# Sixteen prefilled row buffers, weight parts between the transposes, stored rows by the vector engine, and a dense product begun on three tiles

## What is computed

```python
def _gine_layer(x, src, dst, edge_attr, eps, We, be, W1, b1, gamma, beta, W2, b2):
    e = edge_attr @ We + be
    m = jax.nn.relu(x[src] + e)
    agg = jax.ops.segment_sum(m, dst, num_segments=x.shape[0])
    h = ((1.0 + eps) * x + agg) @ W1 + b1
    mu = jnp.mean(h, axis=0)
    var = jnp.mean(jnp.square(h - mu), axis=0)
    h = (h - mu) * jax.lax.rsqrt(var + BN_EPS) * gamma + beta
    h = jax.nn.relu(h)
    return jax.nn.relu(h @ W2 + b2)
...
for l in range(L):
    x = _gine_layer(x, src, dst, edge_attr, eps[l], We[l], be[l], W1[l], b1[l], gamma[l], beta[l], W2[l], b2[l])
```

## Time and profile before

| | |
|---|---|
| median of 3 runs | 971.86 us (967.61 to 972.33) |
| profiled execution | 970.5 us |
| its span on the core | 968.6 us |
| mean granted clock of PE | 0.921 |
| PE busy | 841.4 us, 87% |
| DVE busy | 712.1 us, 74% |
| ACT busy | 516.6 us, 53% |
| POOL busy | 281.5 us, 29% |

### The profile page before, as it was taken

The page is one execution under the profiler, slowest core; times in us unless marked ns, Lnnn a source line. Parts: engine busy times, 40 slices in busy tenths (PEclk is TensorE's granted clock), DMA queues, the critical chain, the costliest instruction groups (busy, mean ns, idle before and its releaser), DMA issues.

```text
span 968.6 us, 13328 instructions
## 1 busy us (share of the span) xinstructions
PE 841.4 (87%) x3561; PEld 603.7 (62%) x3561; DVE 712.1 (74%) x1275; ACT 516.6 (53%) x986; POOL 281.5 (29%) x245
## 2 busy tenths in 40 slices
PE   2989779887869789995999989999999999999796
PEld 2667345655647567773665865667656766658664
DVE  8997825765876677786888668976799758986535
ACT  2376103544646241514786567755677557764445
POOL 3000653865200000015352075502654045520000
PEclk9989657989969799997999999999999999999898
DMA  5412454676433312208676077841978138860101
GB/s 113 142 38 87 115 161 154 178 225 193 151 99 157 129 45 64 84 26 217 148 187 180 3 202 179 200 119 33 240 177 217 37 108 197 178 165 1 43 1 53
DMA packets 59286, 122.20 MB, mean 126 GB/s; under 512 B 9096, under 2 KB 22698, under 8 KB 59221
## 3 DMA queue, kind: packets, MB, share of 16 engines
q0 software_dynamic: 20048, 52.18, 22.6%
q1 hardware_dynamic: 36581, 64.56, 22.6%
q10 hardware_dynamic: 2592, 4.61, 1.3%
HBM read 105.60 MB, written 15.73 MB: 125 GB/s over the span
## 4 chain that ended last, share of the span: by engine, by line
PE 67%; DVE 17%; ACT 8%; issue 5%; another core or an unknown queue 2%; DMA 1%; SPq 0%; ACTq 0%; DVEq 0%
PE ps L996 15%; PE ps L973 10%; PE ps L671 9%; PE ps L1012 6%; PE ps L1028 6%; PE ps L797 4%; PE ps L862 3%; PE ps L919 3%; PE ps L776 2%; PE ps L663 2%; ACT slot_recs L1090 2%; PE ps L765 2%; DVE z_parts L1864 1%; DVE w L1391 1%
## 5 line engine op out<-in xcount | busy, mean ns | idle before, releaser
L996 PE MATMUL ps<-z_parts,onehot_dst 128*125 128x512 f32 x664 | 205.2, 414 | 5.6 <-DVE z_parts L1864 2.9
L1864 DVE SCALAR_TENSOR_TENSOR z_parts<-ps,z_parts 128x512 fp32r<-128x512 f32 x216 | 147.9, 688 | 43.4 <-ACT z_parts L1296 31.0
L671 PE MATMUL ps<-w,xT 128*125 128x512 f32 x660 | 174.7, 419 | 5.1 <-DVE w L1391 5.1
L1296 ACT ACTIVATE z_parts<-ps 128x512 fp32r<-128x512 f32 x216 | 128.7, 597 | 80.9 <-PE ps L973 66.9
L973 PE MATMUL ps<-x_parts,gather_lhs 128*128 x432 | 142.4, 415 | 22.5 <-DVE x_parts L1831 12.1
L996 PEld LDWEIGHTS ps<-z_parts,onehot_dst 128*125 128x125 f32 x664 | 110.0, 186 | 72.8 <-issue 55.0
L671 PEld LDWEIGHTS ps<-w,xT 128*125 128x125 f32 x660 | 129.8, 200 | 37.7 <-issue 6.8
L639 POOL DMA_INDIRECT queued<-node_rows,srci x60 | 96.0, 1600 | 93.7 <-ACT queued L1245 76.8
L653 POOL TENSOR_TENSOR work<-x_cur,be_rows 125x512 f32<-125x512 f32 x20 | 25.5, 1282 | 317.7 <-ACT x_cur L1059 188.9
L973 PEld LDWEIGHTS ps<-x_parts,gather_lhs 128*128 128x128 f32 x432 | 80.3, 193 | 56.5 <-issue 40.2
L633 POOL DMA_INDIRECT gathered<-rel_rows,rowi x79 | 85.7, 1084 | 51.4 <-DVE gathered_parts L1623 22.0
(11 more groups left out here) (275 smaller groups left out, 1154.7 us busy)
## 6 DMA issues: line engine op xcount, KB each, us to landing
w_stage<-in_weights SPq DMA_DIRECT2D x88, 256.0 KB
onehot_dst<-onehot_rows SPq DMA_DIRECT2D x80, 250.0 KB
onehot_rows<-onehot_dst ACTq DMA_DIRECT2D x18, 250.0 KB
gather_lhs<-edge_src_rows SPq DMA_DIRECT2D x8, 432.0 KB, 7.4
node_rows<-work SPq DMA_DIRECT2D x20, 160.0 KB, 2.0
queued<-node_rows,srci POOLq DMA_INDIRECT x116
node_rows<-work SPq DMA_DIRECT2D x20, 90.0 KB, 2.0
rel_rows<-rel_rows_out SPq DMA_DIRECT2D x10, 160.0 KB, 1.9
```

Of the source, the lines that this page charges most:

```text
L671: mm = pe.matmul(ps[0:R, bank, :], lt[:, a, k, n * R:(n + 1) * R], w[:, b, k, :], start=first and k == 0 and (a, b) == THREE[0], stop=last ...
L996: mm = pe.matmul(ps[0:R, d, :], S[:, j // SK % SR, j % SK, :], Z[:, g % ZR, a, :], start=False, stop=False, skip_group_check=True)
L1296: nc.scalar.activation(Z[:, g % ZR, HI, :], of, ACT.Relu).then_inc(z_hi, 1)
L1864: v.scalar_tensor_tensor(out=Z[:, g % ZR, LO, :], in0=of, scalar=0.0, in1=Z[:, g % ZR, HI, :].bitcast(F32), op0=ALU.max, op1=ALU.subtract) ...
```

## The change

It has four parts.

- **Sixteen prefilled buffers.** QR goes from 10 to 16; six more buffers lie in the second half of the adjacency's region, which the third network doesn't use. The first 16 fetched tiles of a layer are all prefilled by ACT and filled by adding DMAs; of the 13 after them every second one. `queue_set` runs 23 times a layer instead of 15, `queue_add` 6 times instead of 14. The sets of buffers 0 and 1 stand in the first dense product (SET_W1), those of 2 to 10 after the cast of the next layer's first weights (SET_W2), those of 11 to 15 at steps 2, 4, 6, 8, 10 of the pass (SET_AT).
- **Second weights among the transposes.** ACT's and DVE's parts of W 13 + 2l leave the pass and are made around the transposes of the last two row tiles. SP's load of W 14 + 2l, which needs their staging buffers, follows; the load of We's next row stands ahead of it.
- **Stored rows by DVE.** From the second layer on DVE writes relu(result) + be into H straight from PSUM, behind each low part; POOL does it only ahead of the first layer. ACT's X copy waits for that instead of for the low part.
- **First dense product begun on three row tiles.** PE transposes three tiles, does the first job, transposes the last two, and goes on.

```diff
-QR = 10
+QR = 16
+QL = 10
...
-EARLY = 10
+SET_W1, SET_W2 = 2, 11
+SET_AT = (2, 4, 6, 8, 10)
...
-W2_HIGH, W2_LOW = (24, 26, 28, 30), (28, 31, 34, 37)
...
-SETS = (TL + 1) // 2
-ADDS = TL // 2
+MIXED = TL // 2
+SETS = QR + (TL - QR + 1) // 2
+ADDS = TL - SETS
...
-        Q = [at(l_at, TF * P * 4 + 2048 * i, f"queued{i}", [P, D]) for i in range(QR)]
-        BEB = at(l_at, TF * P * 4 + 2048 * QR, "be_rows", [P, D])
-        WEB = at(l_at, TF * P * 4 + 2048 * (QR + 1), "we_rows", [P, D])
+        Q = [at(l_at, TF * P * 4 + 2048 * i, f"queued{i}", [P, D]) for i in range(QL)]
+        Q += [at(a_at, APAD * 4 + 2048 * i, f"queued{QL + i}", [P, D]) for i in range(QR - QL)]
...
+        def prefilled(k):
+            return k < QR or (k - QR) % 2 == 0
+
+        def sets(k):
+            return sum(prefilled(j) for j in range(k + 1))
+
+        def adds(k):
+            return k + 1 - sets(k)
...
+                if l < NL2 - 1:
+                    sp.wait_ge(q_set, SETS * (l + 1))
+                    sp.wait_ge(q_add, ADDS * (l + 1))
+                    web_load(l + 1)
                 w_load(14 + 2 * l)
                 if l < NL2 - 1:
                     for g in range(SR):
                         s_load(l + 1, g)
-                    sp.wait_ge(q_set, SETS * (l + 1))
-                    sp.wait_ge(q_add, ADDS * (l + 1))
-                    web_load(l + 1)
...
-                if k % 2 == 0:
-                    gp.wait_ge(q_set, SETS * l + k // 2 + 1)
+                if prefilled(k):
+                    gp.wait_ge(q_set, SETS * l + sets(k))
                     gp.indirect_dma_start(Q[k % QR][:, :], None, xb_d, row, compute_op=ALU.add)\
                         .then_inc(q_in[k % QR], 16)
                 else:
-                    if k >= QR:
-                        gp.wait_ge(z_made, l * TE + STEP[TF + k - QR] + 1)
+                    gp.wait_ge(z_made, l * TE + STEP[TF + k - QR] + 1)
...
+            gp.wait_ge(beb_in, 16)
+            for n in range(NT):
+                gp.wait_ge(x_made, XM_L3 - NT + n + 1)
+                gp.tensor_tensor(H[0:R, n, :], X[0:R, n, :], BEB[0:R, :], ALU.add).then_inc(xb_made, 1)
...
-                for n in range(NT):
+
+                def g_transposes(n):
                     pe.wait_ge(g_made, l * NT + n + 1)
                     transposes(n, H[0:R, n, :])
+
+                for n in range(3):
+                    g_transposes(n)
                 pe.wait_ge(w_split, wpieces(WJ_L2[l]))
                 for i, (o, h) in enumerate(HJOBS):
+                    if i == 1:
+                        g_transposes(3)
+                        g_transposes(4)
...
-                    for k in range(0, EARLY, 2):
+                    for k in range(5):
...
+                for k in range(5 + n + n // 2, 6 + n + (n + 1) // 2 if n < NT - 1 else 0):
+                    queue_set(0, k)
...
-                k = EARLY
+                k = QR
...
+                    if i in SET_AT:
+                        queue_set(l, SET_W2 + SET_AT.index(i))
...
-                    if i in W2_HIGH:
-                        w_high(13 + 2 * l, W2_HIGH.index(i))
-                for n in range(NT):
+                for n in range(3):
                     tr_high(n, GT, n, TR_L2[l] + n + 1)
+                w_highs(13 + 2 * l)
...
+                    if i == 0:
+                        for n in range(3, NT):
+                            tr_high(n, GT, n, TR_L2[l] + n + 1)
                     if i >= 2:
                         (h_high if i % 2 else root_h)((i - 2) // 2)
-                    if l < NL2 - 1 and 2 * i < EARLY:
-                        queue_set(l + 1, 2 * i)
+                    if l < NL2 - 1 and i < SET_W1:
+                        queue_set(l + 1, i)
...
+                    for k in range(SET_W1, SET_W2):
+                        queue_set(l + 1, k)
...
-                            act.wait_ge(xs_made, NT * (l + 1) + n)
+                            act.wait_ge(xb_made, NT * (l + 1) + n)
...
-                k = 1
+                k = QR + 1
...
-                    if i in W2_LOW:
-                        w_low(13 + 2 * l, W2_LOW.index(i))
...
-                for n in range(NT + 2):
-                    if n < NT:
-                        g_tile(n)
-                    if n >= 2:
-                        tr_low(n - 2, GT, n - 2, TR_L2[l] + n - 1)
+                for n in range(3):
+                    g_tile(n)
+                for n in range(3):
+                    tr_low(n, GT, n, TR_L2[l] + n + 1)
+                for n in range(3, NT):
+                    g_tile(n)
+                    w_low(13 + 2 * l, n - 3)
+                for n in range(3, NT):
+                    tr_low(n, GT, n, TR_L2[l] + n + 1)
+                w_low(13 + 2 * l, 2)
+                w_low(13 + 2 * l, 3)
...
+                    v.wait_ge(beb_in, 16 * (l + 2))
                     for n in range(NT):
                         v.wait_ge(xs_hi, NT * (l + 1) + n + 1)
                         v.scalar_tensor_tensor(out=XS[0:R, LO, n, :], in0=ps[0:R, n, :], scalar=0.0,
                                                in1=XS[0:R, HI, n, :].bitcast(F32), op0=ALU.max,
                                                op1=ALU.subtract).then_inc(xs_made, 1)
+                        v.scalar_tensor_tensor(out=H[0:R, n, :], in0=ps[0:R, n, :], scalar=0.0, in1=BEB[0:R, :],
+                                               op0=ALU.max, op1=ALU.add).then_inc(xb_made, 1)
```

35 lines of the change are left out of this document (16 added, 19 removed).

## The result

| | before | after |
|---|---|---|
| median, on one chip | 971.73 us (20 runs) | 975.5 us (20 runs, 968.2 to 983.3) |
| ratio, 95% interval | | 1.0052 (1.003 to 1.0075) |
| span of the profiled execution | 968.6 us | 974.3 us |

A forecast was written before the change was run, and what follows sets the result against it. The tensor engine was taken as head of the chain, with the vector engine's work explaining the slow groups. Gains of 18.5 and 0.8 less losses of 6.9 and 3.7 gave 961.8 us, 962.5 as median; range 951.5 to 971.5.

The forecast's parts named there:

- Groups 0 to 7: First eight five-step groups of each pass: without additions and weights, 4.0 us each instead of 4.58, gaining 18.5 us.
- my lower bound of 12.1: Least gain forecast for groups 0 to 7, if they take 4.20 us each.
- My first rival: In the passes: groups stay at 4.20 us, held by the tensor engine's word reads, not additions; 968.2 us, chance 0.18.
- Switch: Between layers: nine sets in a row delay the high parts, gathers start 2.3 us later three times, 6.9 us lost.
- Clock at the first twelve tiles: Start of three passes: longer idle lowers the clock, 13.55 us for each, 3.7 us lost.
- First dense product: Start of the product after each pass: begun on three tiles, it gains 0.2 us a layer, 0.8 in all.
- Norms: Ahead of the first pass: six more sets lie in scalar engine gaps of some 3 us and cost nothing.
- DMA engines: Rival in the passes: sixteen adding fetches fill the DMA engines, the pass waits for rows; 986 us, chance 0.10.

The follow-up runs named there:

- e5: Changed kernel with LAG = 4: tensor engine scatters a tile four steps after its gather instead of three; ratio to before 0.9844.
- e9: Kernel before with LAG = 4 (scatter four steps after the gather instead of three), nothing else; ratio to before 0.9774.
- e4: Kernel before with the 17 words of bucket numbers read into registers once instead of in every pass; 962.5 us, ratio to before 0.9898.
- e12: Kernel before with LAG = 4 and the words of bucket numbers read once into registers; ratio to before 0.9706.
- e6: Changed kernel with LAG = 4 and the words of bucket numbers read once into registers; ratio to before 0.9772.
- e1: Changed kernel with the nine sets at the layer switch spread over the first dense product; 965.9 us, ratio to before 0.9938.
- e10: Changed kernel with the stored rows made by GpSimd again; 972.7 us beside 973.0 for before, ratio 0.9997.
- e13: Kernel before with only the first dense product begun on three row tiles; 946.8 us beside 950.4 for before, ratio 0.9978.
- e16: e15 with the first dense product begun on three row tiles instead of five; 917.45 us, ratio to before 0.9682.
- e15: Changed kernel with sets spread, dense product begun on five tiles, norms' sets behind the first root, words read once, LAG = 4; 916.74 us, ratio to before 0.965.
- e8: Same kernel as e15, on another chip; 917.85 us, ratio to before 0.9664.
- e2: Changed kernel with the first dense product begun on all five row tiles again; 975.5 us, ratio to before 1.0039.

## Why the prediction was wrong

**Groups 0 to 7 (18.5 us, mis-sized): the step that failed.** "I take 4.0, nearer to the measured group than to the bound": it was 4.29 (4.37 at most in the traces with this pass), the gain 9.1 in the trace, under my lower bound of 12.1. The step before it was wrong in kind. I explained 4.20 and 4.58 by the vector engine's busy sum ("3.0 us a group. On top come one addition"), and so took 3.70, where that sum no longer counts, and 4.20, the group with an addition, for the two ends. But the groups were held by the delay of a tile from gather to scatter, which a sum over an engine does not contain. An addition ahead of a tile lengthens it, and so does a set on the scalar engine, of which the change has more. e5, e9 and the pair of e4 and e12 show it, with one number changed. My first rival had a part of it: the word reads hold 0.06 to 0.14 us a group in the kernel before (e4) and 0.11 to 0.17 in the changed one at LAG = 4 (e5 to e6), the delay 0.2 to 0.4 (e5, e9). In the changed kernel as it was predicted both weigh together, and there their shares are not shown apart. One reading of the rows was off as well: the low parts of the second weights come in groups 3 to 5 of the kernel before, not 2 to 5.

**Switch (6.9 us): right.** Nine sets of 5.63 us, the wait longer by 2.16 us where 2.3 was forecast; e1 takes it back. e10 adds what I had only half said: the sets and DVE's second result are needed together, either one away gives 1.4 to 2.0 us back.

**Clock at the first twelve tiles (3.7 us): right in kind, +1.0 in the two traces.** I took 13.55 us for each of the three; they took 13.07, 13.09 and 12.54 at a granted clock of 0.82 to 0.86, 1.7 more than before and not 3.7, and the lead of the first pass was 0.7 shorter, for which nothing in the record gives a cause. Over all the traces a long wait costs 3.8 us in the mean (39.1 against 35.4), and e1 gives 3.6 back; two of before's three leads behind a switch had been slow already.

**First dense product (gain of 0.8): not seen.** The first job does start 1.2 us sooner, and at full clock the second product 0.25, as forecast. But it may start at half clock, and in the changed kernel's trace that lost 1.25 us in three layers. In the mean of all traces the start on three tiles is 0.16 us a layer later, and e13 and e16 against e15 leave it at nothing within what they can tell.

**Norms ("cost nothing"): 1.0 us in the trace.** The cover was there, but the sets stand ahead of the next tile's root, and the vector engine waits for that. The ratio can't show so little.

**DMA engines (chance 0.10): rightly set aside for this kernel.** The share was 0.91 to 0.94 in the last three windows, and no high part waited for a fetched tile. In e8, where groups 0 to 7 are 12 us faster in sum, the one-hot loads are late.

Put together, the traces differ by +5.7 us where -8.7 was forecast. Of these 14.4 us the groups make 9.4 and the dense product 4.5 (nothing sure in the median); 3.1 are the drift ahead of the norms, and 1.0 the sets in them; groups 8 to 12 and the tails add 0.4; the clock gave 2.7 back, and the stretch behind the last scatter 1.3. The drift has no known cause: over the traces with before at 972 to 974 us the first pass begins anywhere between 447.0 and 452.5 us. Two things stay open. The ratio of e2 is level with the changed kernel's though its trace is 5 us shorter in the place changed; that the changed kernel's trace had all four layers at half clock, where half of them are by the other traces, is a part of the answer. And LAG = 4 took 20 us off the changed kernel by ratio (uncertain by 4.4), of which the groups of the two traces show 13.4.
